# Two Strassen aggregation passes replaced by plain passes over stored fp16 pairs

## The reference, cut to what matters

```python
    h = relu(layernorm(x)); x = x + relu(aug @ h @ W0)              # aug: dinv * (adj + I) * dinv
    h = relu(layernorm(x)); x = x + (a_norm @ h) @ W1.T + b1        # a_norm: dis * adj * dis
    h = relu(layernorm(x)); x = x + relu((A_norm @ h) @ W2)         # A_norm: (adj + I), normalized
    h = relu(layernorm(x))                                          # last layer
    attn_a, attn_b = sigmoid([adj @ h, h] @ Wa.T + ba), sigmoid([adj @ h, h] @ Wb.T + bb)
    e = where(adj != 0, exp(-leaky_relu(s_left[:, None] + s_right[None, :], 0.01)), 0)
    x_a = (e / (sum(e, axis=1) + 1e-5)) @ (h @ W_sa)
    x_b = adj @ (h @ W_gcnb) + b_gcnb
    x = x + sigmoid(attn_a * x_a + attn_b * x_b)
```

## Time and profile before

| | |
|---|---|
| median of 3 runs | 1968.91 us (1967.98 to 1978.61) |
| the profiled execution | 1979.47 us |
| its span, first to last instruction | 1977.7 us |
| TensorE busy | 1772.3 us, 90% |
| VectorE, ScalarE, GpSimd busy | 1170.7, 796.6, 613.5 us |
| moved by DMA | 360.50 MB |

### The profile page before, as it was taken

One profiled execution on the slowest core, in us unless ns is written; L12 is line 12 of the kernel. 1 busy time (PEld: TensorE's weight loads), 2 busy tenths in 40 slices (PEclk: granted clock), 3 DMA queues, 4 the chain that ended last, 5 costly groups with the idle time before them and its releaser, 6 DMA issues.

```text
span 1977.7 us, 25513 instructions
## 1 busy us (share of the span) xinstructions
PE 1772.3 (90%) x9568; PEld 879.1 (44%) x9568; DVE 1170.7 (59%) x2022; ACT 796.6 (40%) x1269; POOL 613.5 (31%) x525
## 2 busy tenths in 40 slices
PE   2789697987789887899899999899999999999998
PEld 0334243444234332345444466544447844444445
DVE  5886585757686775666113234347441167788766
ACT  4664433434444444343102223221110166686656
POOL 0001444423477645242001101023110045454441
PEclk9899898998989998999999999999999999999999
DMA  8865466547577667666865847786574733344332
GB/s 337 344 233 159 146 159 192 150 129 233 150 202 225 187 200 194 152 183 184 315 188 153 255 122 233 267 253 184 171 196 133 238 111 81 103 115 121 110 88 95
DMA packets 293418, 360.50 MB, mean 182 GB/s; under 512 B 31250, under 2 KB 187346, under 8 KB 290074
## 3 DMA queue, kind: packets, MB, share of 16 engines
q1 hardware_dynamic: 293294, 358.87, 59.9%
HBM read 267.63 MB, written 91.16 MB: 181 GB/s over the span
## 4 chain that ended last, share of the span: by engine, by line
PE 50%; DVE 10%; DMA 6%; issue 4%; ACT 4%; POOL 3%; SPq 1%; DVEq 0%; ACTq 0%; POOLq 0%
PE ps L1199 19%; PE ps L1136 10%; PE ps L1179 5%; PE ps L1180 5%; PE ps L1181 5%; DMA RG<-Sd 2%; PE ps L1247 2%; DVE RG L1506 1%; DMA CLd<-HB 1%; DMA HBd<-stage 1%; PE ps L1231 1%; DVE HB L1534 1%; DVE stage L1493 1%; DVE HB L1525 1%; DMA Sd<-HB 1%
## 5 line engine op out<-in xcount | busy, mean ns | idle before, releaser
L1179 PE MATMUL ps<-RG,HB 128*128 128x512 f16 (+1 forms) x1440 | 520.7, 367 | 166.3 <-DVE RG L1506 138.2
L1180 PE MATMUL ps<-RG,HB 128*128 128x512 f16 (+1 forms) x1440 | 518.9, 366 | 0.0
L1181 PE MATMUL ps<-RG,HB 128*128 128x512 f16 (+1 forms) x1440 | 517.8, 365 | 0.0
L1199 PE MATMUL ps<-RG,HB 128*128 128x512 f16 (+1 forms) x2520 | 469.3, 346 | 19.1 <-DMA RG<-Sd 16.9
L1199 PEld LDWEIGHTS ps<-RG,HB 128*128 128x128 f16 x2520 | 247.5, 99 | 232.8 <-DMA RG<-Sd 20.5
L1179 PEld LDWEIGHTS ps<-RG,HB 128*128 128x128 f16 x1440 | 144.0, 100 | 340.4 <-DVE RG L1506 162.3
L1136 PE MATMUL ps<-W,OT 128*128 128x512 f16 (+1 forms) x1272 | 283.9, 380 | 1.0 <-DVE stage L1607 1.0
L2152 POOL TENSOR_TENSOR HB<-HB 128x512 f32<-128x512 f32 (+2 forms) x126 | 169.4, 1345 | 196.7 <-DVE HB L1534 196.7
L1506 DVE SCALAR_TENSOR_TENSOR RG<-RG,cS 128x512 f16<-128x512 f32 (+1 forms) x179 | 148.2, 843 | 125.5 <-ACT RG L1873 125.1
L1181 PEld LDWEIGHTS ps<-RG,HB 128*128 128x128 f16 x1440 | 144.7, 100 | 153.2 <-issue 20.2
L1180 PEld LDWEIGHTS ps<-RG,HB 128*128 128x128 f16 x1440 | 144.3, 100 | 142.2 <-issue 15.9
(11 more groups left out here) (240 smaller groups left out, 2001.0 us busy)
## 6 DMA issues: line engine op xcount, KB each, us to landing
RG<-Sd SPq DMA_DIRECT2D x315, 256.0 KB, 3.1
RG<-in_adjT SPq DMA_DIRECT2D x253, 256.0 KB, 3.2
Sd<-HB SPq DMA_DIRECT2D x100, 320.0 KB, 4.0
HB<-HBd SPq DMA_DIRECT2D x40, 512.0 KB, 5.5
HB<-in_adj SPq DMA_DIRECT2D x14, 1354.0 KB, 7.9
HB<-in_adjT SPq DMA_DIRECT2D x62, 256.0 KB, 4.6
Sd<-RG SPq DMA_DIRECT2D x100, 128.0 KB, 3.3
OT<-in_adj SPq DMA_DIRECT2D x7, 1354.0 KB, 8.0
```

Source lines behind the costliest of these rows:

```text
L1179: eng.matmul(o, h[0], hi, start=j == 0, stop=False)
L1180: eng.matmul(o, h[0], lo, start=False, stop=False)
L1181: last = eng.matmul(o, h[1], hi, start=False, stop=False)
L1199: last = eng.matmul(o, HB[:, slot, JJ, i, b * P:(b + 1) * P], rhs, start=k in PRODUCTS[:3] and JJ == 0 and n == 0, stop=JJ == 9 and n == 2 ...
```

## The change

Passes 2 and 3 become plain passes of six chunks each, so that there are 30 chunks: 12 to 17 are pass 2, 18 to 23 pass 3, 24 to 29 pass 4. Their right operands are the fp16 pairs of pass 1: `a_keep` stores every pair of chunks 6 to 11 in `Ad` (256 KB, one DMA; 74 KB in a narrow chunk, in pieces of 296 bytes), and the diagonal pairs of chunks 2 to 5, which hold the identity, in `Id`. For chunks 0 and 1 the diagonal pairs are made again in pass 1 (`i_sum`, `i_hi`, `i_lo`, 8 tiles) and stay in SBUF (`eyes`). Passes 2 and 3 fetch a pair of 256 KB per unit of 12 matmuls into 10 slots. Everything about block sums, Strassen products and their combinations is gone: `m_*`, `g_*`, `sums`, `neg`, `take`, `out`, `mul`, `left`, `cl`. A Strassen product's projection (`product`) becomes `project`; the projection of a pass's last chunk stands after unit 3 of the next pass. `T` has its own space. Weights get later `w_hi` and `w_lo`, and `norms`, `normed`, `image` and `restore` are placed later too; `stage` holds two images; pass 3's results have four buffers.

```diff
-CHUNKS = [(p, t0, nt) for p in (0, 1, 4) for t0, nt in ROWS]
+CHUNKS = [(p, t0, nt) for p in range(5) for t0, nt in ROWS]
-GE = 12
+GP = 12
+GE = 24
+NPAIR = 10
-SEQ += [("agg", g, j) for g in range(2, GE) for j in range(NT)]
-SEQ += [*strassen_steps(2), *strassen_steps(3)]
-SEQ += [("agg", g, j) for g in range(GE, G) for j in range(NT)]
+SEQ += [("agg", g, j) for g in range(2, G) for j in range(NT)]
+def resident(g, j):
+    return g in (GP, GP + 1) and on_diagonal(g, j)
+def kept(g, j):
+    return 6 <= g < GP or 2 <= g < 6 and on_diagonal(g, j)
+def source(g, j):
+    return (g - 12 if g < 18 and on_diagonal(g, j) else g % 6 + 6), j
+def freed(user):
+    if user is None:
+        return []
+    kind, g, j = user
+    if kind != "raw":
+        return [("agg", g, j)] + ([("a_keep", g, j)] if kind == "sp" and kept(g, j) else [])
     if g >= GE:
+        return [("mask", g, j)]
+    return [("i_lo", g, j) if resident(g + 6, j) and g >= 6 else ("split", g, j)]
...
     def weights(u, n):
-        for d, kind in ((0, "w_fetch"), (3, "w_max"), (4, "w_hi"), (5, "w_lo"), (7, "w_keep")):
+        late = 4 if n in (1, 3, 4) else 2
+        for d, kind in ((0, "w_fetch"), (3, "w_max"), (4 + late, "w_hi"), (5 + late, "w_lo"), (11 + late, "w_keep")):
     def pair(u, l, J):
-        plan(max(later(u, 1.3), u + 1), "norms", l, 2 * J, 2)
-        u = max(later(u, 2.6), u + 1, quiet)
+        plan(max(later(u, 2.6), u + 1), "norms", l, 2 * J, 2)
+        u = max(later(u, 5.2), u + 2, quiet)
+        steps = [(0, "normed", l, 2 * J), (0.6, "normed", l, 2 * J + 1), (1.4, "hi", l, J), (2.7, "lo", l, J)]
+        if J < 8:
+            steps.append((7.9, "image", l, J))
...
+        if g % 6 == 0 and g and j == 3:
+            project(u, g - 1, g)
...
-    for g, J in MAIN:
-        u = AT["agg", g, 2 * J + 1] - 3
-        for i in (0, 1):
-            plan(u + i, "a_keep", g, 2 * J + i)
-        for d, kind in ((0, "m_sum"), (2, "m_hi"), (3, "m_lo"), (4, "m_keep")):
-            plan(u + d, kind, g, J)
+    for _, g, j in SEQ:
+        if g < GP and kept(g, j):
+            plan(AT["agg", g, j], "a_keep", g, j)
+        if 6 <= g < GP and resident(g + 6, j):
+            for d, kind in ((-1, "i_sum"), (0, "i_hi"), (1, "i_lo")):
+                plan(AT["agg", g, j] + d, kind, g, j)
+    for l in (1, 2, 3):
         for slot in range(4):
+            plan(AT["agg", 6 * l - 1, 10], "restore", l, slot, 0)
...
-    plan(u0 + 6, "factors", 0)
+    plan(u0 + 7, "factors", 0)
...
+                    if GP <= g < GE:
+                        sync.wait_ge(*KEPT[source(g, j)])
...
+                            for at_free in slot_free(freed(user_before("pair", g, j))):
+                                sync.wait_ge(*at_free)
+                            eng.dma_start(pairs[:, PAIRSLOT[g, j], :, 0:w],
+                                          home(*source(g, j))).then_inc(s_f[PAIRSLOT[g, j]], 16)
...
                 elif kind == "a_keep":
                     g, j = of
-                    q, i = RING[g, j][1] % NSP, j % 2
                     sync.wait_ge(s_slo, s("split", g, j))
-                    eng.dma_start(home((g, j // 2))[:, 5 + i, :, :], sp[:, q, :, 256 * i:256 * i + 256]).then_inc(s_akept[q], 16)
+                    src = st[0:TK, g % 2, 0:width(g)] if j == NT - 1 else sp[:, SPSLOT[g, j], :, 0:width(g)]
+                    eng.dma_start(home(g, j), src).then_inc(KEPT[g, j][0], 16)
...
-                    pe.wait_ge(*LOADED[key])
-                    if J == 0:
-                        for bank in BANKS[k]:
-                            opened(bank)
-                    for JJ in (J,) if c < 2 else (2 * J, 2 * J + 1):
-                        pe.wait_ge(*h_ready(l, slot, JJ))
-                        for b, bank in enumerate(BANKS[k]):
-                            for n, (i, r) in enumerate(THREE):
...
                     if p == 4:
                         pe.wait_ge(s_elo, s("split_e", g, j))
-                    else:
+                    elif p < 2:
                         pe.wait_ge(s_slo, s("split", g, j))
+                    elif resident(g, j):
+                        pe.wait_ge(s_ilo, s("i_lo", g - 6, j))
+                    else:
+                        pe.wait_ge(*LOADED[g, j])
```

More of the change, by code:

```diff
@@ L71 @@
[L71 to L86, removed]
@@ L89, in main_buffer @@
[L89 to L106, removed]
@@ new lines @@
+for _key in SEQ:
+    _g, _j = _key[1:]
+    if _j == NT - 1:
+        continue
+    if _g < GP or _g >= GE:
+        _n = len(SPSLOT)
+        SPSLOT[_g, _j] = _n % NSP
+        RAWSLOT[_g, _j] = (_n - 2 * (NT - 1)) % (NRAW + NEXTRA) if 2 <= _g < GP else _n % NRAW
+        if RAWSLOT[_g, _j] < NRAW:
+            USERS.setdefault(RAWSLOT[_g, _j], []).append(("raw", _g, _j))
+        else:
+            USERS.setdefault(("x", RAWSLOT[_g, _j]), []).append(("raw", _g, _j))
+        USERS.setdefault(NRAW + SPSLOT[_g, _j], []).append(("sp", _g, _j))
+    elif not resident(_g, _j):
+        PAIRSLOT[_g, _j] = len(PAIRSLOT) % NPAIR
+        USERS.setdefault(PAIRSLOT[_g, _j], []).append(("pair", _g, _j))
@@ L230, in plan, with have @@
         plans.setdefault(u, []).append(stage)
-    def have(stage):
-        return stage is None or stage in s.no
+    def have(*stages):
+        return all(stage in s.no for stage in stages)
     def ahead(u):
@@ L328, in run, with project @@
             put(kind, *a)
+    def project(u, g, now):
+        p = CHUNKS[g][0]
+        put("project", g, now)
+        if p == 4:
+            finals(u + 1, g)
+            return
+        posts(u + 1, p, tiles(g))
+        if p == 3:
+            plan(later(u + 1, 10.4), "gates", g)
+            plan(later(u + 1, 13), "gated", g)
     def step(u):
-        if u == U4:
-            last_products()
         for stage in plans.pop(u, ()):
@@ L443, in schedule @@
-    for slot, k in enumerate(("M2", "M1", "M4", "M5", "M3", "M7", "M6")):
-        plan(AT[LASTSTEP[2, 2, k]] + 1, "restore", 3, slot, 0)
-    plan(U2 + 8, "w_load", 0)
-    plan(U2 + 3, "project", 11, None)
-    posts(U2 + 5, 1, tiles(11))
-    plan(U3 + 24, "w_load", 1)
-    plan(U2 + 30, "bias_load")
-    for l, base in ((2, U2), (3, U3)):
-        for c in range(3):
-            first = AT["mul", l, c, "M2", 0]
-            plan(first, "border", l, c)
-        first = AT["mul", l, 1, "M2", 0]
-        for i in range(8):
-            plan(first + 6 + 3 * i, "product", l, i)
-        first = AT["cl", l, 0]
-        for i in range(5):
-            plan(first + 1 + 2 * i, "product", l, 8 + i)
@@ L477, in schedule @@
+    plan(AT["agg", 12, 12], "w_load", 0)
+    plan(AT["agg", 18, 12], "w_load", 1)
+    plan(AT["agg", 13, 8], "bias_load")
+    plan(AT["agg", 18, 14], "v_load")
+    plan(AT["agg", 18, 18], "bound")
+    plan(AT["agg", 18, 20], "shift")
+    for t in range(NT):
+        u = AT["agg", 19, 0] + 3 * t
+        plan(u, "dot_norm", t)
+        plan(u + 1, "dots", t)
+        plan(u + 2, "xhalf", t)
+    for g in range(GE, G):
+        first = AT["agg", g - 1, 6]
         for i in range(CHUNKS[g][2]):
@@ L846, in proj_done, with slot_free, image_no @@
+        for g, now in in_order("project"):
+            for i, t in enumerate(tiles(g)):
+                p = CHUNKS[g][0]
+                PROJ[p, t] = len(PROJ) + 1
+                BANK[p, t] = i if now is None or p == 4 else 4 - agg_base(now) + i
+        def slot_free(stages):
+            sems = {"agg": s_agg, "split": s_slo, "i_lo": s_ilo, "mask": s_mask}
+            return [KEPT[a[1:]] if a[0] == "a_keep" else (sems[a[0]], s(*a)) for a in stages]
         def proj_done(p, *ts):
             return s_proj, max(PROJ[p, t] for t in ts)
-        def images_before(l, J):
-            return sum(1 for a in s.order[:s.order.index(("hi", l, J))] if a[0] == "image")
+        def image_no(l, J):
+            return 8 * (l - 1) + J
@@ L2127, in _ @@
+                elif kind == "i_sum":
+                    g, j = of
+                    o = (j - CHUNKS[g][1]) * P
+                    part = raw(g, j)[:, o:o + P]
+                    pool.wait_ge(s_slo, s("split", g, j))
+                    eng.tensor_tensor(part, part, identf[:, 0, :], ALU.add).then_inc(s_isum, 1)
                 elif kind == "xbias":
```

1100 lines of the change are left out of this document (247 added, 853 removed).

## The result

The kernel after takes 1884.73 us (median of 4, 1883.33 to 1887.13) against 1970.55 (1967.98 to 1978.61) for the kernel before on the same chip: ratio 0.956, 95% interval 0.953 to 0.959. Forecast: 1893, range 1866 to 1945.

A forecast was written before the change was run, and what follows sets the result against it. Matmuls were taken to bound passes 2 and 3, and splits made late by the block sums passes 0 and 1. -130 + 9 + 33 + 8 = -80 on 1979.5 us gives 1899.5, less some 6 for the median: 1893, range 1866 to 1945.

The forecast's parts named there:

- Term 1: Passes 0 and 1 from the first projection on: 22 us lost in place of 152, so -130 us.
- Term 2: First projection: it waits for the later `w_lo` of weight 0 and restarts at the low clock, +9 us.
- The 22 us that were kept: Passes 0 and 1, surviving waits: 5 us behind all-reduces, 5 behind `restore`, 9 in chunk 11, 3 elsewhere.
- a raw slot is held until GpSimd's sums are made: Passes 0 and 1: the reason given for late splits, with 152 us lost there.
- Chunk 11: Narrow chunk where every pair is stored and its slot waits for the store, over the ring behind four restores: 9 us.
- Term 3: Passes 2 and 3: from 681.8 us to 715 with plain matmuls and few waits, +33 us.
- Small pieces: Rival, chance 0.06: 296-byte pieces make chunks 11, 17 and 23 take 38 us each at worst; 1933 us in all.
- Term 4: Pass 4: pass 3's last projection and its gates move in, the 4.66 us wait stays, +8 us.
- The marks: Signs over the whole kernel: split waits under 40 us, split's mean near 0.77, GpSimd near 260, passes 2 and 3 some 715.
- The splitting stays the pace: Rival, passes 0 and 1, chance 0.20: only half of the 152 us comes back, -26 us, 1943 us.
- The store ring: Rival, pass 1, chance 0.05: splits wait for their slots' stores, +80 us over 105 wide tiles, kernel no longer faster.
- It cancels: Rival, chance 0.05: only 45 of the 152 us in passes 0 and 1 come back, added matmuls eat them; +5, 1974 us.

The follow-up runs named there:

- e1: Kernel after with the 18 block sums of wide chunks 2 to 4 put back, raw slots held: 38.9 us lost over their matmuls, 1925.7 us in all.
- e2: As e1, but GpSimd adds from two tiles that nobody writes, so no raw slot is held: 39.2 us lost in chunks 2 to 4, 1923.4 us.
- e8: Kernel after with the whole weight schedule of the kernel before, without the sums: 1879.5 us, 3.3 us lost in chunks 2 to 4.
- e10: Kernel after with all 18 sums, held slots, halves and stores, and the weight schedule of the kernel before: 43.1 us lost in chunks 2 to 4.
- e6: Kernel after with the restores of narrow chunks 5, 11 and 17 planned 3, 6 and 3 units later: 1873.81 us, ratio 0.947 to the kernel before.
- e5: Kernel after with layer 1's product, halves and factors back at their places of the kernel before: 1875.89 us, ratio 0.948 to the kernel before.
- e7: Kernel after with both the edits of e5 and e6: 1865.36 us, ratio 0.943 to the kernel before.

## Why the prediction was right

- **Term 1** (-130, measured -133.6, or -135.1 without the slow projection that term 2 holds). The price of 216 ns a matmul held: wide chunks without a wait take 55.3 us for the 55.4 forecast. The 22 us that were kept came out as 17.5: behind the all-reduces 1.9 instead of 5, chunk 5 4.3 instead of 5, chunk 11 11.9 instead of 9, the rest nothing instead of 3. The step that failed is the reason: "a raw slot is held until GpSimd's sums are made" costs nothing that can be seen in chunks 2 to 4 (e1 against e2, 38.9 and 39.2 us). The other half of the sentence, that VectorE slows down while GpSimd adds, was given one row and is the largest single part, 11.5 us of the 37.6 in three chunks; GpSimd's queue in front of the all-reduce takes 8.5, the halves 6.6, the stores 6.6, and having adds and halves together 4.4. The sum came out because all parts left with the same edit, whichever was the cause: as to the reason, that was luck. It would have been wrong for a change that frees the slots and keeps the sums.
- That nothing of the 10.7 us wait of unit (2, 15) is kept was right, and for two reasons, each enough alone: the later `w_hi`, as the prediction says (e1 has the sums and no wait there), and the missing sums (e8 has the early `w_hi` and no wait there). With both the wait is back, 11.0 us (e10).
- **Chunk 11**: the size was near, the place right, "over behind the four restores". e6 shows that the restores make 7.8 us of the 11.9 over the price of 17; the rest stays open.
- **Term 2** (+9). Wait 5.6 us for 5.7 forecast, by the steps as given: VectorE's evacuation from 177.86, 2.48 us, then the 2.34 us lo half. The low clock cost 1.5 for 3. Chunk 1 also ended 1.3 us sooner, which e5 and e8 (projection at 178.4 and 178.0) show to be within what one execution differs from the next.
- **Term 3** (+33, measured +30.2). The pass borders cost nothing, for 2; chunk 17 cost 5 over its 16.4 without a wait (e7), for 3. Small pieces did not pace the narrow chunks: chunk 17 in 16.4 us (e6) can't be reconciled with 38. The Trainium skill ("DMA: Bandwidth & Descriptors", Specifications) says that pieces under 512 bytes lose line rate, and the prediction put 1956 us beside it. The trace shows no loss at this pace, one fetch of 74 KB in 0.75 us a unit; what rate such pieces reach at most no run here shows.
- **Term 4** (+8, measured +6.7). The wait of the earlier trace rows is there again, 4.7 us.
- **The sum** was 12 us short of the change between the two profiled executions, and 6 short against the medians (85.8): 5 from term 1, 3 from term 2, 3 and 1 from the others, all on the same side. The forecast of the median, 1893, was 8 us too high. The rivals' 1943 and 1974 are counted from the median of 1968.9 itself and the forecast from some 4 us above it, a slip that changes no verdict.
- **The marks.** Waits for splits "under 40" were 49.6: the forecast forgot the start's 35.5 in both lists; without it they are 14.1. The split's mean was 713 ns for 770, GpSimd 268.5 us for 260, pass 2 to pass 4 712 us for 715.
- **Rivals.** "The splitting stays the pace" is refuted by the 55.3 us of wide chunks in both passes. So are "The store ring", for wide chunks, and "It cancels": the wide chunks of pass 1 store every pair and take 55.3 us.

Not settled: e10 rebuilds 43.1 of the 52.6 us; 6.5 of the missing 9.5 are in chunk 4. The kernel before also stored pairs of 128 KB in chunks 2 to 4 and had another buffer layout; neither was tested. From the projection after chunk 5 to pass 2, where 75.8 us of the gain lie (448.8 before, 373.0 after), nothing was put back; that the same causes hold there is an analogy, and the held slot, behind GpSimd's waits for its stores, may count there.

## What to carry to other kernels

Before moving an elementwise sum to an idle GpSimd, look at what VectorE does in the same stretch: if its instructions read two operands from SBUF, they get slower while GpSimd reads too (817 to 1040 ns a split here). When an edit takes away several suspects at once, its total can be forecast well from the idle time that it opens, but not its reason; put the suspects back one by one before the reason is used for the next kernel. Large transfers with slack belong behind the small ones without it: moving four fetches of 512 KB by six units was worth 8 us in one narrow chunk.

## What the runs showed of the hardware that was not expected

GpSimd shows 6 to 7 us without any instruction before a weight's all-reduce and 7 to 8 us after it, in each timeline above (5.91 and 7.57 us, of which the first is put down to VectorE's maximum; 6.46 and 7.15; 6.63 before it in e10), while the reduce itself shows 0.38 us. A VectorE split of 128x512 takes 817 ns beside no sums, 812 beside memsets of 128x1280 and 1040 beside adds. A store of 74 KB that was issued right behind four fetches of 512 KB landed after 7.64 us, against a median of 2.5 for such stores.
